# A two-pass cross-attention layer in float32: last denominators on VectorE, low-rank products in row groups, a key fold in the head

## The chip, the core and the metric

The kernel runs on one core of a Trainium2 chip. The core has five engines with queues of their own: TensorE (PE) multiplies matrices, VectorE (DVE) and ScalarE (ACT) work element by element and read TensorE's results from PSUM (8 banks of 128 x 512 float32), GpSimd (POOL) does small element work, and SyncE (SP) issues most of the DMA. They wait for each other through semaphores. The metric is the device time of one execution in microseconds.

## The reference

x is 128 latent rows of 256. The context has 12544 rows of 256. In float32:

```
x = x + cross_attention(layernorm(x), ctx)      # 16 heads of 64
    q = LN(lat) Wq;  k, v = LN(ctx) Wkv
    p = softmax(clip(q k^T / 8, -11, 11));  out = (p v) Wo + bo
x = x + self_attention(layernorm(x))            # 16 heads of 16
    Q, K, V and the output: y W^T + b + 2 (y A^T) B^T, A and B of rank 8
x = x + ffn(layernorm(x))                       # row-scaled fp8 values times fp8 weights
```

Nearly all the work is the cross-attention of the 128 latent rows with 12544 context rows.

## The kernel before

**Cross-attention.** The context is cut into 98 key tiles of 128 rows, 49 pairs. The 16 heads are done in two passes of 8 (`PASSES`), each over all pairs (`passes`, L266). Pair 0 and pairs 41 to 48 are written out, pairs 1 to 40 are a loop. Weights are folded once with the layer norm: for keys, Wk is folded (`key_fold`, L520) and multiplied with q to `qk_hi` and `qk_lo`; for values `value_fold`. Every float32 operand is split in a high and a low part, so a product is three matmuls (`mm3`, L456). A step is one key tile: on TensorE `values`, two times `scores`, and `weighted_sum` of the tile before (L488); ScalarE takes the exponentials (`exps`), VectorE clips them (`clip`), ScalarE and VectorE make their high and low parts (`p_high`, `p_low`), and VectorE adds them to `den` (`add_den`, L1021).

**Side work.** Steps of pairs 41 to 48 carry one extra piece each, numbered by `step_of` (L278). In pass 0 these make the second half's weights: key folds (`KEY_STEPS`), products with q (`QK_STEPS`), value folds (`VALUE_STEPS`). In pass 1 they project pass 0's heads, and one (`LORA_STEP`) scales the low-rank A. Before the passes stands the head: loads, layer norm of x, the first half's folds, the first tile.

**The end.** Behind the last tile, `denominators` (L506) turns `den` and the last tile's `ex` into one column per head: matmuls with a 128 x 128 stationary operand and a single moving column. `save` adds the high and low sums on VectorE (L1159), `inverse` takes the reciprocals (L1163), `project` multiplies each head with Wo (L516), and `add_head` adds the scaled result to x1 on VectorE (L1170), each addition waiting for the one before. Self-attention then needs the weights W + 2 B A: an identity matmul `weights_plain` (L662) puts W in PSUM and `weights_lora` (L668) adds the low-rank product; ScalarE copies the result (`effective_weights`, L911). Then: normalised rows (`hn`, L969), their transposes (L696), q and k (`projected`, L680), scores (L715, four row groups), exponentials (L920, L924), transposes (`transposed_probs`, L726), v projection (L734), products with v (L744), output projection (L757), and the fp8 layer. VectorE decodes the fp8 weights in between (`fp8_weights`).

The order on every engine is the order in which the code is written; no scheduler changes it.

Of the kernel before, what the change touches and what calls it, by code (L numbers as in the profile page):

```python
# [23 lines left out]
def perceiver_layer(  # L24
# [30 lines left out]
    with ExitStack() as stack:  # L55
# [13 lines left out]
        WO_BANK = (bank[4], bank[5], v_bank, side_bank)  # L69
# [67 lines left out]
        aa_all = sb("aa_all", [R, 4 * D])  # L137
        aa = [aa_all[:, n * D:(n + 1) * D] for n in range(4)]
        abT = [sb(f"abT{n}", [R, D]) for n in "qkvo"]
# [120 lines left out]
        AW_BANK = (3, 0, 3, 2)  # L260
# [22 lines left out]
        KEY_STEPS, QK_STEPS, VALUE_STEPS = range(0, 2), range(2, 6), range(6, 8)  # L283
        DEN_STEP, WO_STEPS, LORA_STEP = 0, range(1, 1 + HP), 1 + HP
# [21 lines left out]
        def _(sp):  # L306
# [39 lines left out]
            for n, (w, a, b_) in enumerate(((aWq, aAq, aBq), (aWk, aAk, aBk), (aWv, aAv, aBv), (aWo, aAo, aBo))):  # L346
                late_loads += [(aw[n][:, :, :], rows(w)), (aa[n], a), (abT[n][:, :], b_)]
# [107 lines left out]
        def _(pe):  # L455
# [50 lines left out]
            def denominators(dst, by_head, start, stop):  # L506

                for h in range(HP):
                    ins = pe.matmul(dst[:, h:h + 1], by_head[:, h, :], ones_sq[:, 0:1], start=start and h == 0,  # L509
                                    stop=stop and h == HP - 1)  # L510
                if stop:
                    ins.then_inc(s_denp, 1)

# [81 lines left out]
            pe.wait_ge(s_qT, CH + 1)  # L595

            def pair(p, i, phase):
                gp = p * PAIRS + i
                static = isinstance(i, int)
                for b in range(2):  # L600
# [19 lines left out]
                    if p == 0 and extra in KEY_STEPS:  # L620
                        if extra == 0:
                            pe.wait_ge(s_wk[1], 16)
# [680 lines left out]
```

## Time and profile before

| | |
|---|---|
| median of 3 runs | 1081.56 us (1081.37 to 1081.64) |
| profiled execution | 1076.75 us, its span 1075.0 us |
| busy in the span | TensorE 99%, VectorE 86%, ScalarE 61%, GpSimd 16% |
| mean granted clock of TensorE | 0.995 of 2.4 GHz |

How to read it: one execution was recorded. Times count from the start of the span. A timeline row gives start, length, engine, line, operation, output and inputs, and in brackets the idle time before it with what ended it. "x8" is eight instructions merged; a float32 matmul of the program is two instructions here, a transpose one. Matmuls overlap and their ends are modelled, so the pace of a run is read from starts, or from the chain of waits, which counts each stretch of time once.

### The profile page before, as it was taken

How to read it: one execution, taken by the hardware profiler on the slowest of the kernel's cores; microseconds unless marked ns; L12 is line 12 of the kernel's file. 1: busy time of each engine (PE TensorE's matmuls, PEld its weight loads, DVE VectorE, ACT ScalarE, POOL GpSimd, SP SyncE). 2: the span in 40 equal slices, each digit the busy share in tenths (PEclk: the TensorE clock that was granted, in tenths of full speed). 3: DMA queues.
4: the chain of work that ended last, by engine and by line, in shares of the span. 5: the costliest groups of instructions: out<-in, count | busy, mean ns of one | idle time of the engine just before them, and what ended most of it. 6: DMA issues, size and time to landing. Idle time of an engine off the chain costs nothing.

```text
span 1075.0 us, 18235 instructions
## 1 busy us (share of the span) xinstructions
PE 1065.5 (99%) x5510; PEld 906.0 (84%) x5510; DVE 926.8 (86%) x1321; ACT 660.8 (61%) x934; POOL 171.6 (16%) x213
## 2 busy tenths in 40 slices
PE   8999999999999999999999999999999999999998
PEld 6888888888888888888888888888888888888876
DVE  4999999999999999888888888888888888888864
ACT  4666666666666666565666666666666666666632
POOL 3233233233232232212000000000000000000000
PEclk9999999999999999999999999999999999999998
DMA  5321221221222212221151111111111111110000
GB/s 181 114 75 49 73 73 49 73 69 53 73 61 61 73 56 66 87 73 43 50 123 45 29 44 44 29 44 43 30 44 38 35 44 33 41 44 16 1 1 5
DMA packets 52509, 58.78 MB, mean 55 GB/s; under 512 B 31170, under 2 KB 32772, under 8 KB 52356
## 3 DMA queue, kind: packets, MB, share of 16 engines
q1 hardware_dynamic: 52052, 57.80, 18.5%
q10 hardware_dynamic: 432, 0.66, 0.2%
q8 instruction: 14, 0.23, 0.1%
q14 instruction: 11, 0.09, 0.0%
HBM read 58.20 MB, written 0.13 MB: 54 GB/s over the span
## 4 chain that ended last, share of the span: by engine, by line
PE 98%; DVE 1%; ACT 0%; issue 0%; POOL 0%; DVEq 0%; POOLq 0%
PE wide L458 25%; PE wide L459 25%; PE wide L460 25%; PE wide L499 17%; PE wide L516 1%; PE wide L523 1%; PE wide L530 1%; PE wide L509 0%; PE wide L545 0%; PE wide L551 0%; PE wide L538 0%; PE wide L744 0%; PE wide L680 0%; PE wide L668 0%; PE wide L726 0%; PE wide L662 0%
## 5 line engine op out<-in xcount | busy, mean ns | idle before, releaser
L816 ACT ACTIVATE ex<-wide,c_rstd 128x512 f32<-128x512 f32 x392 | 270.3, 690 | 201.3 <-PE wide L460 200.2
L458 PE MATMUL wide<-qk_hi,d_hi 128*128 128x512 f32 x784 | 305.2, 389 | 0.0
L460 PE MATMUL wide<-qk_hi,d_lo 128*128 128x512 f32 x784 | 305.0, 389 | 0.0
L459 PE MATMUL wide<-qk_lo,d_hi 128*128 128x512 f32 x784 | 305.0, 389 | 0.0
L1018 DVE TENSOR_TENSOR ph<-ex,ph 128x1024 fp32r<-128x1024 f32 x195 | 239.0, 1225 | 73.7 <-ACT ph L823 73.6
L823 ACT CAST ph<-ex 128x1024 fp32r<-128x1024 f32 x195 | 205.3, 1053 | 148.6 <-DVE ex L1000 148.6
L1027 DVE TENSOR_TENSOR den_all<-den_all,ex 128x1024 f32<-128x1024 f32 x193 | 234.6, 1215 | 0.0
L499 PEld LDWEIGHTS wide<-ph,vhl 128*128 128x128 f32 x1568 | 212.7, 190 | 16.6 <-DVE ph L1018 2.1
L499 PE MATMUL wide<-ph,vhl 128*128 128x256 f32 x1568 | 218.9, 282 | 0.0
L458 PEld LDWEIGHTS wide<-qk_hi,d_hi 128*128 128x128 f32 x784 | 147.1, 188 | 31.8 <-DVE qk_lo L1032 0.3
L459 PEld LDWEIGHTS wide<-qk_lo,d_hi 128*128 128x128 f32 x784 | 147.2, 188 | 30.8
L460 PEld LDWEIGHTS wide<-qk_hi,d_lo 128*128 128x128 f32 x784 | 147.1, 188 | 30.5
L1000 DVE TENSOR_SCALAR ex<-ex 128x1024 f32<-128x1024 f32 x195 | 135.1, 693 | 33.7 <-ACT ex L816 25.2
L458 PE MATMUL wide<-wv_hi,d_hi 128*128 128x512 f32 x392 | 158.3, 404 | 1.7 <-DVE vhl L989 1.7
L459 PE MATMUL wide<-wv_lo,d_hi 128*128 128x512 f32 x392 | 154.7, 395 | 0.0
L460 PE MATMUL wide<-wv_hi,d_lo 128*128 128x512 f32 x392 | 152.7, 390 | 0.0
L989 DVE SCALAR_TENSOR_TENSOR vhl<-wide,c_rstd,vhl 128x512 fp32r<-128x512 f32 x196 | 146.0, 745 | 3.1 <-ACT vhl L809 3.1
L809 ACT ACTIVATE vhl<-wide,c_rstd 128x512 fp32r<-128x512 f32 x196 | 133.6, 681 | 6.3 <-PE wide L460 6.0
L411 POOL TENSOR_TENSOR sig_all<-c_veps,half_pow 128x2 f32 (+1 forms) x49 | 46.0, 939 | 357.3 <-DVE c_veps L980 357.3
L417 POOL COPY c_rstd<-rstd_all 128x2 f32 (+1 forms) x49 | 26.7, 545 | 458.9 <-ACT ex L816 458.9
L460 PEld LDWEIGHTS wide<-wv_hi,d_lo 128*128 128x128 f32 x392 | 73.7, 188 | 17.0
L458 PEld LDWEIGHTS wide<-wv_hi,d_hi 128*128 128x128 f32 x392 | 74.3, 190 | 12.6 <-issue 2.6
(163 smaller groups left out, 636.0 us busy)
## 6 DMA issues: line engine op xcount, KB each, us to landing
t_all<-in_ctxT_dram SPq DMA_DIRECT2D x98, 384.0 KB, 3.1
x_pair<-in_ctx_dram SPq DMA_DIRECT2D x49, 256.0 KB, 2.7
diff<-sig_all SPq DMA_DIRECT2D x194, 0.5 KB, 1.9
wkv<-in_Wo_dram SPq DMA_DIRECT2D x2, 1024.0 KB, 10.1
wq<-in_Wq_dram SPq DMA_DIRECT2D x2, 512.0 KB, 7.7
wkv<-in_Wv_dram SPq DMA_DIRECT2D x2, 512.0 KB, 6.5
wkv<-in_Wk_dram ACTq DMA_DIRECT2D x1, 512.0 KB, 4.7
wkv<-in_Wk_dram SPq DMA_DIRECT2D x1, 512.0 KB, 3.6
```

What stands on the lines that cost most here:

```text
L411: pool.tensor_tensor(sig_all[:, pair_cols], c_veps[s][:, :], half_pow[:, :], ALU.pow).then_inc(s_sig, 1)
L458: pe.matmul(dst, hi, mhi, start=start, stop=False)
L459: pe.matmul(dst, hi, mlo, start=False, stop=False)
L460: return pe.matmul(dst, lo, mhi, start=False, stop=stop)
L499: ins = pe.matmul(acc[m][:, a, :, :], vhl[b][:, 2 * m + a, :, :].rearrange("p n d -> p (n d)"), ph[b][:, place(m, a), :, :], start=start a ...
L809: act.activation(vhl[b][:, :, 0, :], v_bank[:, :].rearrange("p (h d) -> p h d", h=HP), ACT.Identity, scale=c_rstd[s4][:, b:b + 1]).then_in ...
L816: act.activation(ex[b][:, c * HC:(c + 1) * HC, :], sc_bank[c][:, :].rearrange("p (h q) -> p h q", h=HC), ACT.Exp, scale=c_rstd[s4][:, b:b ...
L823: act.copy(ph[b][:, :, 0, :], ex[b][:, :, :]).then_inc(s_phi, 1)
L989: dve.scalar_tensor_tensor(vhl[b][:, :, 1, :], v_bank[:, :].rearrange("p (h d) -> p h d", h=HP), c_rstd[s4][:, b:b + 1], vhl[b][:, :, 0, : ...
L1000: dve.tensor_scalar(ex[b][:, :, :], ex[b][:, :, :], EXP_LO, EXP_HI, ALU.max, ALU.min).then_inc(s_clip, 1)
L1018: dve.tensor_tensor(ph[b][:, :, 1, :], ex[b][:, :, :], ph[b][:, :, 0, :].bitcast(F32), ALU.subtract)\
L1027: dve.tensor_tensor(den[p], den[p], ex[b][:, :, :], ALU.add).then_inc(s_den, 1)
```

## The change

- **Head.** `key_fold(1, CHUNK_M[0], side_bank)` and ScalarE's `key_weights` for it move from the first extra step of pass 0 to the end of the head; the load of Wk's second half moves in front of the sigma rows on SP. All later extra steps of pass 0 come one step earlier.
- **Denominators.** VectorE adds the last tile's `ex` to `den[1]` in two halves (`add_den_last`), and TensorE does 8 one-column matmuls, 4 ahead of and 4 behind the last weighted sum. The identity matmul for the q weights is issued ahead of them.
- **Low-rank products.** The A and B of q, k, v and o lie on partitions 0, 32, 64 and 96, and all eight matmuls are issued together behind the projections, for bank 7, 1, 2 and 3; the identity matmuls of k, v and o add to them later. A is scaled by four small operations in four steps.
- **Banks and order.** The last projections go to banks 4, 5, 6, 0 and 4 again (`WO_DST`); the v projection comes before the transposes of the probabilities; `save` comes before `inverse`; the fp8 decoding comes behind VectorE's copies of the transposes.

TensorE at the end of the program, before, from the last weighted sum but one (L499) over denominators (L509), projections (L516), identity matmuls (L662) and low-rank products (L668) to q and k (L680):

```order
L499 MATMUL wide<-ph,vhl 128x256 x8
L509 MATMUL wide<-ones_sq,den_all 128x1 x8
L509 MATMUL wide<-ones_sq,ex 128x1 x8
L499 MATMUL wide<-ph,vhl 128x256 x8
L516 MATMUL wide<-wkv,osum 128x256 x8
L662 MATMUL wide<-awq,ident 128x512
L668 MATMUL wide<-abTq,aa_all 128x256 x2
L662 MATMUL wide<-awk,ident 128x512
L696 MATMUL wide<-ident,ex 128x128 x2
L668 MATMUL wide<-abTk,aa_all 128x256 x2
L680 MATMUL wide<-latT,x_pair 128x128 x8
```

The same place after (weighted sums L498, denominators L508, projections L521, low-rank products L672, identity matmuls L514, q and k L685):

```order
L498 MATMUL wide<-ph,vhl 128x256 x8
L514 MATMUL wide<-awq,ident 128x512
L508 MATMUL wide<-ones_sq,den_all 128x1 x4
L498 MATMUL wide<-ph,vhl 128x256 x8
L508 MATMUL wide<-ones_sq,den_all 128x1 x4
L521 MATMUL wide<-wkv,osum 128x256 x8
L672 MATMUL wide<-abT_all,aa_all 128x256 x8
L514 MATMUL wide<-awk,ident 128x512
L703 MATMUL wide<-ident,ex 128x128 x2
L514 MATMUL wide<-awv,ident 128x512
L685 MATMUL wide<-latT,x_pair 128x128 x8
L514 MATMUL wide<-awo,ident 128x512
```

Half of the one-column matmuls are gone and the rest stand on both sides of the weighted sum; the low-rank products are one group of eight, and the first identity matmul stands ahead of the denominators.

VectorE at the same place, before: clips (L1006), low parts of the probabilities (L1013), inverse, saves, heads (L1170):

```order
L1027 TENSOR_TENSOR den_all<-den_all,ex 128x1024
L1006 TENSOR_SCALAR ex<-ex 128x512 x2
L1013 TENSOR_TENSOR ph<-ex,ph 128x4x128 x2
L1163 RECIPROCAL rden<-wide 128x8
L1159 TENSOR_TENSOR osum<-osum,wide 128x2x128 x4
L1170 SCALAR_TENSOR_TENSOR x<-wide,rden,x 128x256 x8
```

After: clips (L1009), denominator additions (L1024), low parts (L1016), saves, inverse, heads (L1183):

```order
L1037 TENSOR_TENSOR den_all<-den_all,ex 128x1024
L1009 TENSOR_SCALAR ex<-ex 128x512 x2
L1024 TENSOR_TENSOR den_all<-den_all,ex 128x512
L1016 TENSOR_TENSOR ph<-ex,ph 128x4x128 x2
L1024 TENSOR_TENSOR den_all<-den_all,ex 128x512
L1172 TENSOR_TENSOR osum<-osum,wide 128x2x128 x4
L1176 RECIPROCAL rden<-wide 128x8
L1183 SCALAR_TENSOR_TENSOR x<-wide,rden,x 128x256 x8
```

Two additions of half the heads are new, one ahead of the low parts and one behind; the inverse stands behind the saves.

TensorE in the head, before, at the end of the first tile's values:

```order
L458 MATMUL wide<-wv_hi,d_hi 128x512
L459 MATMUL wide<-wv_lo,d_hi 128x512
L460 MATMUL wide<-wv_hi,d_lo 128x512
L458 MATMUL wide<-wv_hi,d_hi 128x512
L459 MATMUL wide<-wv_lo,d_hi 128x512
L460 MATMUL wide<-wv_hi,d_lo 128x512
```

After, with a key fold (L528) there:

```order
L457 MATMUL wide<-wv_hi,d_hi 128x512
L458 MATMUL wide<-wv_lo,d_hi 128x512
L459 MATMUL wide<-wv_hi,d_lo 128x512
L528 MATMUL wide<-foldT,wkv 128x256 x4
L457 MATMUL wide<-wv_hi,d_hi 128x512
L458 MATMUL wide<-wv_lo,d_hi 128x512
L459 MATMUL wide<-wv_hi,d_lo 128x512
```

The fold's four matmuls stand between the first and the second tile's values. ScalarE at this place, before:

```order
L788 ACTIVATE qT<-wide 128x512
L809 ACTIVATE vhl<-wide,c_rstd 128x8x64
L803 CAST d_hi<-diff 128x512
L823 CAST ph<-ex 128x8x128
L809 ACTIVATE vhl<-wide,c_rstd 128x8x64
L816 ACTIVATE ex<-wide,c_rstd 128x512 x2
```

After:

```order
L791 ACTIVATE qT<-wide 128x512
L812 ACTIVATE vhl<-wide,c_rstd 128x8x64
L806 CAST d_hi<-diff 128x512
L787 COPY wkE<-wide 128x512
L826 CAST ph<-ex 128x8x128
L812 ACTIVATE vhl<-wide,c_rstd 128x8x64
L819 ACTIVATE ex<-wide,c_rstd 128x512 x2
```

The copy of the folded weights (L787) stands ahead of the cast of the first probabilities.

The diff, cut to its core:

```diff
-        WO_BANK = (bank[4], bank[5], v_bank, side_bank)
+        WO_DST = [bank[n][:, a * D:(a + 1) * D] for n, a in ((4, 0), (4, 1), (5, 0), (5, 1), (6, 0), (6, 1), (0, 0), (4, 0))]
+        aa_all, abT_all = (sb(n, [P, D]) for n in ("aa_all", "abT_all"))
+        aa, abT = ([t[32 * n:32 * n + R, :] for n in range(4)] for t in (aa_all, abT_all))
-        AW_BANK = (3, 0, 3, 2)
+        AW_BANK = (7, 1, 2, 3)
-        KEY_STEPS, QK_STEPS, VALUE_STEPS = range(0, 2), range(2, 6), range(6, 8)
-        DEN_STEP, WO_STEPS, LORA_STEP = 0, range(1, 1 + HP), 1 + HP
+        KEY_STEP, QK_STEPS, VALUE_STEPS = 0, range(1, 5), range(5, 7)
+        DEN_STEP, WO_STEPS, LORA_STEPS = 0, range(1, 1 + HP), range(1 + HP, 5 + HP)
...
+            sp.dma_start(wkv[:, 0, 1, :, :], Wk[:, 1, :, :]).then_inc(s_wk[1], 16)
             for n in range(1, 3):
                 sp.wait_ge(s_sig, n + 1)
                 sp.wait_ge(s_diff, n + 1)
                 sigma_row(n % 2, n)
-            sp.dma_start(wkv[:, 0, 1, :, :], Wk[:, 1, :, :]).then_inc(s_wk[1], 16)
...
             pe.wait_ge(s_qT, CH + 1)
+            pe.wait_ge(s_wk[1], 16)
+            key_fold(1, CHUNK_M[0], side_bank)
...
                     if ended:
+                        pe.wait_ge(s_late, LATE)
+                        weights_plain(0, True)
                         pe.wait_ge(s_vlo, ALL)
-                        pe.wait_ge(s_den, ALL - 1)
-                        denominators(v_bank, den[1], True, False)
-                        pe.wait_ge(s_clip, ALL + 1)
-                        denominators(v_bank, ex[b], False, True)
+                        pe.wait_ge(s_den, ALL)
+                        denominators(v_bank, den[1], 0)
                     weighted_sum(gp, b, first, last, saved=p * MH if first else 0, ended=ended)
+                    if ended:
+                        pe.wait_ge(s_den, ALL + 1)
+                        denominators(v_bank, den[1], 1)
...
+            def weights_lora():
                 for k in range(KD):
+                    for n in range(4):
+                        ins = pe.matmul(bank[AW_BANK[n]][:, k * D:(k + 1) * D], aa[n][:, k * P:(k + 1) * P], abT[n],
+                                        start=(k == 0 and n > 0), stop=(k == KD - 1 and n == 0))
...
                 for a in range(2):
-                    project(1, m, a, WO_BANK[m][:, a * D:(a + 1) * D])
+                    if (m, a) == (MH - 1, 1):
+                        pe.wait_ge(s_x1, 1 + HP + 2)
+                    project(1, m, a, WO_DST[2 * m + a])
...
+            def add_den_last(c):
+                heads = slice(c * HC, (c + 1) * HC)
+                dve.wait_ge(s_clip, ALL + c)
+                if c == 0:
+                    dve.wait_ge(s_den, ALL - 1)
+                dve.tensor_tensor(den[1][:, heads, :], den[1][:, heads, :], ex[1][:, heads, :], ALU.add).then_inc(s_den, 1)
...
+                        add_den_last(0)
                         p_low_last(g, b)
+                        add_den_last(1)
...
-            inverse(1, v_bank)
             save(PASSES - 1)
+            inverse(1, v_bank)
```

## Rows read from the trace of the kernel before

**Rows 1.** Table of stretches: us, busy and instructions by engine, clock, DMA share, GB/s.
```profile
100.00:1000.00 900.00, 900.00 (x4626) 768.30 (x4625) 796.56 (x1086) 572.79 (x798) 140.60 (x166) 1.00 0.19 53
1031.00:1036.00 5.00, 4.79 (x43) 4.59 (x41) 2.50 (x7) 2.10 (x6) 0.00 (x0) 1.00 0.01 3
1036.20:1039.50 3.30, 3.30 (x9) 2.55 (x9) 1.62 (x4) 0.04 (x1) 0.00 (x0) 0.50 0.00 0
1039.60:1046.30 6.70, 5.81 (x21) 3.37 (x21) 4.82 (x14) 0.59 (x1) 0.56 (x1) 1.00 0.00 1
1046.40:1049.70 3.30, 3.30 (x15) 2.92 (x14) 1.43 (x5) 1.21 (x3) 0.00 (x0) 0.50 0.00 0
1063.50:1066.80 3.30, 3.30 (x14) 2.94 (x13) 0.84 (x2) 0.00 (x0) 0.00 (x0) 0.50 0.00 0
```

**Rows 2.** Timeline, TensorE, 436 to 458: start, length, engine, line, operation.
```profile
440.95 1.12 PE L499 MATMUL wide<-ph,vhl 128*128 128x256 f32 x8
...
446.01 1.12 PE L499 MATMUL wide<-ph,vhl 128*128 128x256 f32 x8
...
452.82 1.11 PE L499 MATMUL wide<-ph,vhl 128*128 128x256 f32 x8
```

**Rows 3.** Timeline of the head, 24 to 29 us.
```profile
24.56 0.40 PE L460 MATMUL wide<-wv_hi,d_lo 128*128 128x512 f32 x1
...
26.09 1.05 ACT L823 CAST ph<-ex 128x1024 fp32r<-128x1024 f32 x1
...
26.69 0.47 PE L458 MATMUL wide<-wv_hi,d_hi 128*128 128x512 f32 x1 [1.73 <-DVE vhl L989]
...
28.60 1.21 DVE L1018 TENSOR_TENSOR ph<-ex,ph 128x1024 fp32r<-128x1024 f32 x1
```

**Rows 4.** SP's timeline, then the view of line 314, 0 to 30 us.
```profile
6.67 0.48 SPq L314 DMA_DIRECT2D t_all<-in_ctxT_dram  x1
...
DMA to landing us min/median/max: 7.6/9.1/10.0
```

**Rows 5.** Chain of waits from 1028 us: start, length, engine, tile, line.
```profile
1031.19 3.47 PE wide L509 x32
...
1035.92 5.42 PE wide L516 x16
...
1042.08 0.49 DVE x L1170
...
1042.69 0.50 DVE x L1170
...
1045.19 0.44 PE wide L696 x2
1045.62 1.23 PE wide L668 x4
1046.85 3.41 PE wide L680 x16
...
1051.12 1.08 PE wide L715 x16
...
1057.67 1.02 PE wide L726 x8
1058.69 3.48 PE wide L744 x32
```

**Rows 6.** Timeline at the last pair's end, VectorE and ScalarE.
```profile
1030.68 0.75 DVE L1006 TENSOR_SCALAR ex<-ex 128x512 f32<-128x512 f32 x2
...
1031.84 1.29 DVE L1013 TENSOR_TENSOR ph<-ex,ph 128x512 fp32r<-128x512 f32 x2 [0.41 <-ACT ph L830]
...
1035.04 1.20 ACT L838 COPY osum<-wide 128x256 f32<-128x256 f32 x4 [2.71 <-PE wide L499]
...
1035.44 1.41 DVE L1159 TENSOR_TENSOR osum<-osum,wide 128x256 f32<-128x256 f32 x4 [0.54 <-ACT osum L838]
```

**Rows 7.** Timeline of ScalarE, 1056.5 to 1058.6.
```profile
1056.74 0.67 ACT L924 ACTIVATE wq<-wq 128x512 f32<-128x512 f32 x1
```

More of the change, by code:

```diff
@@ L504, in weighted_sum, with denominators, weights_plain @@
                     ins.then_inc(s_pv, 1)
[L506 to L511, printed above, removed]
-                    ins.then_inc(s_denp, 1)
+            def denominators(dst, by_head, c):
+                for h in range(c * HC, (c + 1) * HC):
+                    ins = pe.matmul(dst[:, h:h + 1], by_head[:, h, :], ones_sq[:, 0:1], start=(h == 0), stop=(h == HP - 1))
+                if c == CH - 1:
+                    ins.then_inc(s_denp, 1)
+            def weights_plain(n, first):
+                ins = pe.matmul(bank[AW_BANK[n]][:, :], ident[:, :], aw[n][:, :, :].rearrange("p k d -> p (k d)"),
+                                start=first, stop=not first)
+                if not first:
+                    ins.then_inc(s_awp[n], 1)
             def project(p, m, a, dst):
@@ L644, in pair @@
                         pe.wait_ge(s_wvlo, KD * PASSES)
-                        denominators(side_bank, den[0], True, True)
+                        for c in range(CH):
+                            denominators(side_bank, den[0], c)
                     if p == 1 and extra in WO_STEPS:
@@ L718, in _ @@
                         ins.then_inc(s_ascore, 1)
-            weights_lora(2)
-            weights_plain(3)
-            weights_lora(3)
+            pe.wait_ge(s_awE[2], 1)
+            for k in range(KD):
+                pe.matmul(bank[1][:, 0:D], hT[:, k, :], awE[2][:, k, :], start=(k == 0), stop=False)
+            pe.matmul(bank[1][:, 0:D], ones_row[:, :], abv_row[:, :], start=False, stop=True).then_inc(s_avp, 1)
             def transposed_probs(n):
@@ L729, in _ @@
             transposed_probs(0)
+            pe.wait_ge(s_av, 1)
             transposed_probs(1)
-            pe.wait_ge(s_awE[2], 1)
-            pe.wait_ge(s_aexp, 1)
-            for k in range(KD):
-                pe.matmul(bank[4][:, 0:D], hT[:, k, :], awE[2][:, k, :], start=(k == 0), stop=False)
-            pe.matmul(bank[4][:, 0:D], ones_row[:, :], abv_row[:, :], start=False, stop=True).then_inc(s_avp, 1)
             pe.wait_ge(s_awE[3], 1)
@@ L928, in _ @@
             effective_weights(1)
+            effective_weights(2)
             act.wait_ge(s_aqp, 1)
             for m in range(KD):
-                ins = act.activation(aqT[:, m, :], bank[1][:, (2 + m) * P:(3 + m) * P], ACT.Identity,
+                ins = act.activation(aqT[:, m, :], bank[5][:, m * P:(m + 1) * P], ACT.Identity,
                                      bias=abq_col[:, m:m + 1], scale=1.0)
             ins.then_inc(s_aqT, 1)
+            effective_weights(3)
             self_exp(0)
-            effective_weights(2)
-            self_exp(1)
-            self_exp(2)
-            effective_weights(3)
-            self_exp(3)
             act.wait_ge(s_avp, 1)
             act.wait_ge(s_const, 6)
-            act.copy(av[:, :, 0:AD], bank[4][:, 0:D].rearrange("p (h d) -> p h d", h=AH)).then_inc(s_av, 1)
+            act.copy(av[:, :, 0:AD], bank[1][:, 0:D].rearrange("p (h d) -> p h d", h=AH)).then_inc(s_av, 1)
+            for n in range(1, 4):
+                self_exp(n)
             act.wait_ge(s_apTp, 3)
```

68 lines of the change are left out of this document (29 added, 39 removed).

## The prediction

> **What bounds the kernel now.** I read first the table of stretches. From 100 to 1000 us TensorE is busy for every microsecond at the full clock, so in the loops only work taken off TensorE counts [rows 1]. In the last 45 us the same view shows two other things: TensorE is not always busy, and its granted clock falls to 0.50 (1.2 instead of 2.4 GHz) in three stretches [rows 1]. Then the chain of waits of the tail, for what lies on the path there: the denominators (32 instructions, 3.47 us), the last projections (5.42), a chain of additions on VectorE, the wait for the normalised rows, the q and k projections (3.41), the scores, the transposes and the products with v (3.48) [rows 5]. Last the timeline, at the two places where instructions are moved: the head at 24 to 29 us [rows 3] and the end of the last pair of key tiles [rows 6].
>
> **The key fold in the head.** A step of the loop takes 446.01 - 440.95 = 5.06 us, and one that also carries a key fold 452.82 - 446.01 = 6.81 [rows 2]. So one fold costs 1.75 us, 0.219 for each of its 8 instructions, and with one step fewer in pass 0 this goes from a stretch that TensorE bounds. In the head the fold is put where TensorE stands still: the last values matmul starts at 24.56, so its successor could go at about 24.79, and the next one starts at 26.69, released by VectorE's `vhl` [rows 3]. That is 1.90 us for 1.75 us of work. ScalarE has one copy more there, about 0.6 us (half of the 1.20 us of four small copies is the nearest in size [rows 6]; bound 1.05, the large cast [rows 3]), in front of the cast of the first probabilities. The cast ran from 26.09 to 27.14; behind the fold's end (26.6) and the copy it runs from about 27.3 to 28.35, and VectorE asks for it only at 28.60 [rows 3]. So the head costs 0 (between -0.2, as a matmul that starts without a pause saves its ramp, and +0.2). The fold needs the second half of Wk in the head. Its load is put before the sigma rows in SP's queue, behind a load issued at 6.67; the slowest of the loads there took 10.0 us to land [rows 4]. Issued at 7.2 it lands by 17 to 18, against 24.8 when it is needed, and the sigma rows behind it have until 25.6. If that cover failed, TensorE and behind it ScalarE would wait. **Term 1: -1.75.**
>
> **The last denominators.** Now 32 instructions take 3.47 us, before the weighted sum can go [rows 5]. The change adds the last tile's exponentials on VectorE, so 16 stay, 1.74 us, in two halves around the weighted sum. Ahead of them goes an identity matmul (2 instructions, 0.86 us, as the chain has between q/k at 1050.26 and the scores at 1051.12 [rows 5]). VectorE: both clips end at 1031.43; an addition of half the heads is taken at 0.65, half of the 1.29 us of the two subtractions of the same size; it ends at 1032.08, the two subtractions at 1033.37, the second addition at 1034.02 [rows 6]. The subtraction thus comes 0.24 later than its 1031.84, which TensorE doesn't see. TensorE: identity matmul 1031.1 to 1032.0, first half of the denominators 1032.1 to 1032.97, weighted sum (8 instructions, 1.12 with the modelled end [rows 2], so 0.98) to 1033.95, second half 1034.07 to 1034.94. Before, the weighted sum started at 34.66. ScalarE's copies of the sums start 0.38 behind that start, now 1033.36; VectorE's four additions (1.41 [rows 6]) now wait for its second denominator addition, 1034.02 to 1035.43, ahead of TensorE all the same. Queued behind that addition on VectorE are the saves, the inverse and all heads, so it is what sets the pace if TensorE is quick.
>
> **The projections.** They took 5.42 us for 16 instructions, because 3.3 us of them ran at half clock [rows 1, 5]; at 0.219 they take 3.50. The first pair is then done at 1035.82, and VectorE's eight additions to x follow at one per 0.61 us (1042.08 to 1042.69 [rows 5]): 1035.95 + 7 x 0.61 + 0.50 = 1040.75. Before, the last one ended at 1042.69 + 0.50 = 1043.19. **Term 2: -2.4** at full clock; without the clock it is bounded by the order of the work alone, -1.0 (start of the projections 1035.92 to 1034.94). The wait of the last projection for bank 4 costs nothing: two additions are over long before.
>
> **The low-rank products.** Sixteen instructions on 8 rows go at once in four row groups. Alone, four in one group take 1.23 [rows 5]; sixteen with 32 rows in four groups take 1.08 in the scores [rows 5]. Taken: 1.1 for all, bound above by 16 x 0.27 = 4.3 if they don't overlap. TensorE is through with projections at 1038.4, with these at 1039.7 and with the next identity matmul at 1040.6, while the normalised rows come at 1045.19 - 2.4 = 1042.75. So they are hidden; at 4.3 the transposes would be 0.9 late. The late loads and the scaling of A are long done in either kernel, and the four small scalings lie in steps where VectorE has room.
>
> **From the rows to the scores.** Now from 1045.19 to 1051.12 + 1.08 = 1052.20, 7.0 us: the low-rank product 1.23 stands in it, and q and k take 3.41 at half clock [rows 1, 5]. After: transposes 0.44, identity matmul 0.86, q and k 16 x 0.108 = 1.73 (pace of 3.47/32), identity matmul 0.86, scores 1.08: 4.97. VectorE's k halves (0.9) fit beside the identity matmul. **Term 3: -2.0**; at half clock again only -0.3.
>
> **From the scores to the products with v.** Now 58.69 - 52.20 = 6.5, and the last exponential ends at 1057.41 [rows 7], 5.2 behind the scores. The v projection no longer stands before the last transposes (their eight take 1.02 [rows 5], four 0.5). So the products start 5.7 behind. **Term 4: -0.8.** The fp8 decoding moves behind VectorE's copies of the transposes, beside the products, for which VectorE only waits. Its five 512-wide operations take at most 0.65 each, as the subtractions [rows 6], 3.2 in all, and start about 0.6 behind the products' start: nothing, at most 0.3 late.
>
> **The clock takes a part back.** In before, the clock stood low behind the one-column denominators, behind the wait for the normalised rows with a low-rank product, and from 1063.4 on behind the 17-column products [rows 1, 5]. The first two causes get smaller. The third gets larger: the products now follow transposes of 0.5 us with gaps for the exponentials between them, where identity and low-rank products stood. I take the low clock to begin in the middle of the products: some 17 of 32 at 0.213 (3.41/16) instead of 0.109, +1.8, and +0.7 as the short chain behind them is low throughout. **Term 5: +2.5**, bounds 0 and +4.4 (all 32 low: 3.3, and 1.1 behind them).
>
> TensorE: Matmul & The Clock Gate in the Trainium skill (HAM oscillation) puts the fall of the clock down to TensorE standing idle between bursts. By that rule the idle here, which stays short, would leave the products at full clock, and the sum without term 5 would be -7.0. The trace does not agree: the clock was low from 1063.5 behind 3.48 us of products without a pause [rows 1, 5].
>
> **Sum:** -1.75 - 2.4 - 2.0 - 0.8 + 2.5 = -4.5 us. Against the profiled execution's 1076.75 (span 1075.0, 1.75 around it) this is 1072.3. The median of the runs, 1081.56, lies 4.8 above the profiled one; I take the difference as the same in both kernels: 1077.1.
>
> **Rivals.**
> - The clock holds. No low stretch before or in the products: -7.0, 1074.6. For it: half of the one-column work goes, and the denominators stand apart. Against: the products alone brought it down in before. 17%.
> - More low clock than I take: low from the last exponentials through the end of the chain (+4.4), and perhaps also at the projections (+1.4): gain 1.2 to 2.6, 1079.0 to 1080.4. For it: in the softmax TensorE does only four pieces of 0.5 us in 4 us, and once low, thin products don't raise the clock. 21%.
> - The row groups don't overlap: the transposes 0.9 late, 1078.0. Against: the scores' 1.08 for sixteen. 5%.
> - The change doesn't do what it says in the head: Wk lands late, or ScalarE's copy pushes the probabilities, and term 1 is gone: 1078.8. 6%.
> - Slower than before: the gap before the normalised rows grows from 0.9 to 2.1 us (1040.6 to 1042.75). If the clock falls there and, with thin work after it, does not rise before the end, everything TensorE does there runs at half pace: transposes to scores about 9.8 (+2.8 against before's 7.0), the products 6.8 (+3.3), the chain behind them +1.1, in all +7.2, against terms 1 and 2 and 0.3 left of term 4, -4.5: +2.7, 1084.3. It decides from where the low clock takes 4.5 us more than it does in before. Against: dense work raised the clock after each low stretch here. 3%.
> - The forecast, with the low stretch somewhere between q/k and the end of the products (a low stretch on q and k costs 1.7 and spares the products a part of theirs, which comes to nearly the same time): 48%, own range 1075.5 to 1078.5.
>
> **Numbers.** 1077.1. The range takes in most of the clock's cases, 1074.4 to 1080.1. 0.2%, about what a measurement of this kernel can tell from no change, is 2.2 us, so faster means under 1079.4: forecast 48, clock holds 17, row groups 5, head 5, and two thirds of the second rival 14, 89 in all; same 8; slower 3.
>
> **What would show it.** Steps of pass 0: one of 6.81 instead of two. Head: TensorE without the pause at 24.8 to 26.7, and no later start of the first weighted sum. Tail: sixteen one-column instructions in two groups of 0.9; the projections at 0.22 each and clock 1.00; the last addition to x 2.4 earlier relative to the last pair; all low-rank products in 1.1; q and k in 1.73; the products with v partly at 0.21 each. Wrong is the forecast if the clock is 0.50 in the projections, or if the products with v are wholly at one clock.

## The result, and the profile after

| | before | after |
|---|---|---|
| median of the runs in the first comparison (us) | 1081.46 (4 runs, 1080.22 to 1081.64) | 1074.30 (4 runs, 1071.72 to 1075.77) |
| ratio | | 0.9934 [0.9911, 0.9956] |
| median in a second comparison (us) | 1080.41 (21 runs, 1077.02 to 1081.79) | 1076.42 (5 runs, 1074.62 to 1077.57) |
| ratio | | 0.9956 [0.9942, 0.9969] |
| first profiled execution (us), its clock | 1076.75, 0.995 | 1071.72, 0.996 |
| second profiled execution (us), its clock | 1080.32, 0.991 | 1076.47, 0.991 |

The change makes the kernel faster by 7.2 us in the comparison that the forecast was made for, and by 4.0 in the second. The forecast, 1077.1, is 2.8 above the 1074.3 of the first, and the range's low end, 1074.4, is 0.1 above it. The 1076.42 of the second comparison lies inside the range.

Both kernels vary by more than that from one execution to the next. All 9 executions of after lie between 1071.72 and 1077.57, median 1075.77; all 57 of before between 1076.75 and 1081.84, median 1080.81. Over all of them the gain is 5.0. The time goes with the granted clock: of the 41 executions of before that stand beside the experiments below, those at 0.989 and 0.990 took 1081.3 to 1081.8, those at 0.991 1080.1 to 1081.0, those at 0.992 1079.0 to 1080.0, the one at 0.993 took 1078.70 and the one at 0.995 1077.02. At the same granted clock the two kernels can be compared without it: at 0.991 before took 1080.1 to 1081.0 and after 1076.4 to 1077.6, at 0.993 1078.7 (2 runs) and 1074.6 to 1075.8 (4 runs), at 0.995 1076.8 and 1077.0 against 1073.3. That is about 3.5 us for the work alone; what a median shows beyond it comes from which executions it was taken over.

First the steps of the prediction, in after's first profiled execution. Timeline of TensorE in the two kernels, before and then after: the first weighted sum of the program, and the first one of the last pair of tiles.

```profile
30.86 1.11 PE L499 MATMUL wide<-ph,vhl 128*128 128x256 f32 x8
...
1030.07 1.12 PE L499 MATMUL wide<-ph,vhl 128*128 128x256 f32 x8
```

```profile
30.98 1.12 PE L498 MATMUL wide<-ph,vhl 128*128 128x256 f32 x8
...
1028.55 1.12 PE L498 MATMUL wide<-ph,vhl 128*128 128x256 f32 x8
```

The loops are 1.64 us shorter, by the fold that is gone from them; the head is 0.12 longer. What hides the fold there, on all engines of after [rows 3]:

```profile
24.72 0.39 PE L459 MATMUL wide<-wv_hi,d_lo 128*128 128x512 f32 x1
...
24.95 1.89 PE L528 MATMUL wide<-foldT,wkv 128*128 128x256 f32 x8
...
26.75 0.50 PE L457 MATMUL wide<-wv_hi,d_hi 128*128 128x512 f32 x1
...
27.41 1.05 ACT L826 CAST ph<-ex 128x1024 fp32r<-128x1024 f32 x1
...
28.75 1.21 DVE L1028 TENSOR_TENSOR ph<-ex,ph 128x1024 fp32r<-128x1024 f32 x1
```

The values matmul behind the fold starts at 26.75 (26.69 before). ScalarE's cast starts 1.32 later than before and still ends at 28.46, before VectorE asks for it at 28.75. The fold costs the head nothing.

The chain of waits of after's tail [rows 5]:

```profile
1030.67 1.02 PE wide L508 x8
1031.69 1.06 PE wide L498 x8
1032.75 0.79 PE wide L508 x8
1033.54 5.26 PE wide L521 x16
...
1040.12 0.49 DVE x L1183
...
1042.61 0.44 PE wide L703 x2
1043.05 0.86 PE wide L514 x2
1043.91 1.78 PE wide L685 x16
1045.69 0.86 PE wide L514 x2
1046.56 1.11 PE wide L722 x16
...
1053.36 3.48 PE wide L747 x32
...
1059.79 1.53 PE wide L760 x4
...
1067.35 0.48 DVE lat L1263
```

Half the one-column matmuls are gone, 1.02 and 0.79 us stand on both sides of the weighted sum, and q and k (L685) take 1.78 instead of 3.41. But the projections (L521) still take 5.26, as before's 5.42: they are at half clock again. The products with v (L747) are at full clock. The table of stretches of after says the same (us, busy and instructions of TensorE, its weight loads, VectorE, ScalarE and GpSimd, clock, DMA share, GB/s) [rows 1]:

```profile
100.00:1000.00 900.00, 900.00 (x4625) 768.26 (x4624) 798.40 (x1089) 573.46 (x799) 142.16 (x166) 1.00 0.19 53
1033.80:1037.00 3.20, 3.20 (x9) 2.57 (x8) 1.18 (x4) 0.00 (x0) 0.00 (x0) 0.50 0.00 0
1037.20:1057.40 20.20, 17.04 (x121) 11.99 (x119) 13.56 (x33) 7.28 (x18) 0.55 (x1) 1.00 0.00 1
1057.60:1060.90 3.30, 3.30 (x14) 3.03 (x14) 0.42 (x1) 0.00 (x0) 0.00 (x0) 0.50 0.00 0
```

Two low stretches are left before the final chain where before had three: the one on the low-rank product and q/k is gone. The timeline of VectorE in after [rows 6]:

```profile
1029.84 0.68 DVE L1024 TENSOR_TENSOR den_all<-den_all,ex 128x512 f32<-128x512 f32 x1
1030.44 1.29 DVE L1016 TENSOR_TENSOR ph<-ex,ph 128x512 fp32r<-128x512 f32 x2
1031.64 0.68 DVE L1024 TENSOR_TENSOR den_all<-den_all,ex 128x512 f32<-128x512 f32 x1
1032.48 1.41 DVE L1172 TENSOR_TENSOR osum<-osum,wide 128x256 f32<-128x256 f32 x4 [0.15 <-ACT osum L841]
```

The added operations take 0.68 each (0.65 was taken) and the saves run beside TensorE. The sixteen low-rank products, in TensorE's timeline of after, the line that answers to the 1.23 us for four [rows 5]:

```profile
1038.72 1.15 PE L672 MATMUL wide<-abT_all,aa_all 8*128 8x256 f32 x16
```

They do overlap: 1.15 for all sixteen.

Now the same kernel, executed again. Its stretches:

```profile
1042.30:1045.60 3.30, 3.30 (x16) 3.22 (x16) 0.00 (x0) 1.21 (x3) 0.00 (x0) 0.50 0.00 0
1045.70:1052.30 6.60, 5.22 (x36) 2.90 (x34) 5.11 (x11) 3.67 (x11) 0.00 (x0) 1.00 0.00 1
1052.50:1066.10 13.60, 13.60 (x58) 12.37 (x57) 4.32 (x11) 1.03 (x2) 0.00 (x0) 0.50 0.00 1
```

and of its chain of waits the first ten projections (all sixteen took 3.70 in the timeline), q and k, and the products:

```profile
1033.40 2.28 PE wide L521 x10
...
1042.80 3.19 PE wide L685 x16
...
1054.11 6.64 PE wide L747 x32
```

The code is the same, and the time is 1076.47 instead of 1071.72. Here the projections are at full clock, q and k and all the products at half. In before the low stretches began at the same three places in both profiles; in after no low stretch belongs to a fixed instruction. From start to start of the same steps, in the two pairs of profiled executions:

| us | first pair | second pair | forecast |
|---|---|---|---|
| up to the last pair's first weighted sum | -1.52 | -1.92 | -1.75 |
| from there to the end of the additions to x | -1.05 | -2.15 | -2.4 |
| to the end of the scores | -1.96 | -1.93 | -2.0 |
| to the start of the products with v | -0.80 | -0.37 | -0.8 |
| from there to the end | +0.31 | +2.54 | +2.5 |
| sum | -5.02 | -3.83 | -4.45 |

The second pair is close to the forecast line by line, but in part by luck: the forecast was worked out from before's first execution, and before's second one has longer low stretches. Against the first one the second execution of after has -0.32 in the third row and +4.3 in the fifth, which are the prediction's values for q and k at half clock (-0.3) and for low clock from the products to the end of their chain (+4.4). In the first pair the low clock lay in the projections, so the second row is 1.35 short of the forecast, and not in the products, so the last row costs 2.2 less. The two misses cancel in part.

### The profile page after: what moved, and what is told of

Its sections match the earlier page's. It is cut to its first block, busy times and chain, and to the rows that moved or that the text cites. A ratio compares the mean times of both kernels' runs of the same rounds, so it can differ in the third digit from the quotient of the medians.

```text
span 1070.0 us, 18208 instructions
## 1 busy us (share of the span) xinstructions
PE 1059.8 (99%) x5494; PEld 901.2 (84%) x5494; DVE 928.6 (87%) x1326; ACT 660.9 (62%) x934; POOL 173.0 (16%) x213
## 4 chain that ended last, share of the span: by engine, by line
PE 97%; DVE 2%; ACT 0%; issue 0%; POOL 0%; DVEq 0%; POOLq 0%
PE wide L457 25%; PE wide L458 25%; PE wide L459 25%; PE wide L498 17%; PE wide L521 1%; PE wide L528 1%; PE wide L535 1%; PE wide L550 0%; PE wide L556 0%; PE wide L543 0%; PE wide L508 0%; PE wide L747 0%; DVE a_max L1222 0%; PE wide L680 0%; PE wide L685 0%
## 5 line engine op out<-in xcount | busy, mean ns | idle before, releaser
L498 PEld LDWEIGHTS wide<-ph,vhl 128*128 128x128 f32 x1568 | 212.6, 190 | 16.7 <-DVE ph L1028 2.1
L498 PE MATMUL wide<-ph,vhl 128*128 128x256 f32 x1568 | 219.0, 282 | 0.0
```

The costliest lines, as they stand in the source:

```text
L498: ins = pe.matmul(acc[m][:, a, :, :], vhl[b][:, 2 * m + a, :, :].rearrange("p n d -> p (n d)"), ph[b][:, place(m, a), :, :], start=start a ...
```

## Experiments: two executions of each kernel, and the two halves of the change

Before, unchanged.

> The kernel before, unchanged, to see its executions with their clocks. The profiled executions of the two kernels differ by 5.0 us, the medians by 7.2, so 2.1 us lie between executions. Clock theory: executions of one kernel differ by how many low-clock stretches fall on TensorE's work; each lowers the mean granted clock by about 0.0016 and costs up to 1.7 us, so a time of 1081.5 goes with a clock near 0.992 and one of 1077 with 0.995, and its trace shows low stretches that the first profiled execution did not have. Rival (a fixed cost outside TensorE's clock, in loads or in the head): times spread by the same amount with the clock the same.

Measured: 1080.43 (11 runs, 1078.35 to 1081.76) beside 1080.41, ratio 0.9996 [0.9987, 1.0005]. The profiled execution took 1080.32, 3.57 more than the first. Its low stretches:

```profile
1036.00:1039.20 3.20, 3.02 (x7) 2.48 (x8) 1.83 (x6) 0.50 (x2) 0.00 (x0) 0.50 0.00 0
1046.20:1052.80 6.60, 6.60 (x21) 4.36 (x20) 2.62 (x9) 1.21 (x3) 0.00 (x0) 0.50 0.00 0
1063.30:1069.90 6.60, 6.60 (x23) 5.55 (x24) 1.11 (x3) 0.00 (x0) 0.00 (x0) 0.50 0.00 0
```

They begin where the first profile's did [rows 1], but the second and the third last twice as long. So the clock theory's account of the spread held, with 0.990 instead of 0.992 for the executions at 1081.5. The first profiled execution of before was the fastest of all 57; 44 of the 57 are above 1080. The forecast rests on it.

After, unchanged.

> The changed kernel, unchanged. Clock theory: executions from 1071.5 to 1076, each on one line of time against mean clock (0.996 to 0.993, about 1.1 us for 0.001), and a trace with another number of low stretches than the first, or with them at other places; median 1074.3, 7.2 below before. Rival (the gain is all work taken off the path, 7 us, and the first pair of profiles was a poor pair): the trace shows the parts of work adding up to 7 without regard to the clock.

Measured: 1076.42 (5 runs), ratio 0.9956 [0.9942, 0.9969]; its rows are above. The expected median of 1074.3 was missed by 2.1, and one execution, 1077.57, lies above the expected span. The profiled execution stood 2.6 below its own median in the first comparison and at its median in the second.

Only the head's edit, with the load of Wk's second half, in before.

```diff
+            key_fold(1, CHUNK_M[0], side_bank)      # TensorE, end of the head
+            key_weights(CH, CHUNK_M[0], side_bank)  # ScalarE, end of the head
-        KEY_STEPS = range(0, 2)
+        KEY_STEP = 0
```

> The kernel before with only the key fold moved into the head. By steps of the loop -1.75, by the first pair of profiles -1.5: 1.5 to 1.8 us faster than before at the same clock. Rival (the fold is not hidden in the head): 0 faster. If it moves by more than 2, the moved phase of the tail against the clock's stretches has a share.

Measured: 1078.88 (11 runs, 1078.38 to 1079.67), ratio 0.9986 [0.9977, 0.9995]: -1.5, close to the 1.75 of term 1. From the first weighted sum to the last pair's it takes 997.59 us, as after (997.57 and 997.56), against 999.21 and 999.34 in before.

Only the tail's edits: after with the fold and the load of Wk's half back in their old places.

```diff
-            key_fold(1, CHUNK_M[0], side_bank)
-        KEY_STEP, QK_STEPS, VALUE_STEPS = 0, range(1, 5), range(5, 7)
+        KEY_STEPS, QK_STEPS, VALUE_STEPS = range(0, 2), range(2, 6), range(6, 8)
```

> The changed kernel with the key fold put back into the loop, so only the tail is changed. The work theory gives the rest of the gain: 7.2 - 1.6 = 5.6 below before in the median, 3.5 below at equal low stretches. If tail and head don't add up to the whole (within 0.7 us), the clock's phase decides the rest.

Measured: 1076.97 (5 runs, 1076.17 to 1078.89), ratio 0.9964 [0.9951, 0.9978]: -3.4. The expected 5.6, which came from the first comparison's 7.2, was missed; the 3.5 expected at equal low stretches fits. The halves add up to -5.0 where the whole gives -4.0 in the same comparison. The missing 1.0 is less than the 3.0 between the executions of after there, so it says nothing of the two edits getting in each other's way.

## Experiments: can the low clock be taken away?

If the clock makes the difference between executions, a kernel in which it stays high must be faster and vary less, with the same work on the path. Four kernels, all made from after.

Denominators 64 columns wide instead of 1.

```diff
-                    ins = pe.matmul(dst[:, h:h + 1], by_head[:, h, :], ones_sq[:, 0:1], ...)
+                    ins = pe.matmul(dst[:, h * DH:(h + 1) * DH], by_head[:, h, :], ones_sq[:, 0:DH], ...)
```

> The changed kernel; the denominator matmuls move 64 columns of ones instead of one (64 equal results a head, one is read). The pace of such a float32 instruction is 0.109 us with 1 or with 128 columns, so no work is added to the path. Clock theory (thin matmuls bring the clock down): the low stretch that the first profiled execution of the changed kernel had in the projections (1033.6 to 1037.0) does not occur in any execution; in the executions where it did not fall there anyway nothing changes. Median 0 to 1 us below the changed kernel (1075.8 over nine executions), fastest not changed. Rival (only idle time brings it down): no difference.

Measured: 1075.82 (6 runs, 1071.90 to 1077.47), ratio 0.9945 [0.9929, 0.9961]. The eight instructions take about as long as with one column (1.08 and 1.02). The profiled execution (1076.55) has no low stretch in the projections, but one from 1042.5 and then this one:

```profile
1052.80:1066.40 13.60, 13.60 (x57) 12.27 (x56) 4.31 (x12) 0.82 (x2) 0.00 (x0) 0.50 0.01 1
```

These are the places of after's second execution, which has one-column denominators. The medians of that one, 1076.42, and of this kernel differ by less than either spreads: alone this edit brings nothing that shows. Whether the low stretch in the projections is gone from every execution, as the clock theory has it, one profile can't tell.

The products with v also wider, 32 columns a head instead of 17 (the rest are ones, not read).

```diff
-                ins = pe.matmul(bank[5][:, h * (AD + 1):(h + 1) * (AD + 1)], a_pT[:, at, :], av[:, h, :], ...)
+                ins = pe.matmul(bank[5][:, h * 2 * AD:(h + 1) * 2 * AD], a_pT[:, at, :], av[:, h, :], ...)
```

> As den_wide, and the products with v move 32 columns instead of 17 (the rest are ones; not read). Clock theory: the products hold the clock a little better, 0 to 2 us on the median, since in the second profiled execution of the changed kernel the low clock lay over all of them (1052.5 to 1066.3). Rival: as den_wide.

Measured: 1073.04, but from 1070.12 to 1077.49 in 5 runs, ratio 0.9922 [0.9909, 0.9935]. The profiled execution is the slowest of the five, and its clock fell twice: from 1040.1 to 1047.0, beginning while TensorE waited for the normalised rows and lying on q and k (3.41 us), and from 1053.8 to 1067.5, so from the end of the softmax, in which TensorE also waits, and ahead of the wide products. Of its chain:

```profile
1055.12 6.67 PE wide L747 x32
```

The median is 2.8 below that of the kernel with wide denominators alone, but the intervals of the two ratios overlap.

Fillers: after's shapes, with products of the identity with itself that nobody reads where TensorE waits ahead of the products with v, written to a bank that is free there: 5 (10 instructions) ahead of the normalised rows, and 1 or 2 between the transposes of the probabilities. The helper `busy` for them is in both kernels already, with 2, 2 and 16 of them behind the products with v. The identity matmul for the k weights is also held back here until the sixth addition to x.

```diff
+            pe.wait_ge(s_x1, 1 + HP + 6)
             weights_plain(1, False)
+            busy(bank[6], 5)
             pe.wait_ge(s_hn, 1)
...
+            busy(bank[2], 2)
             transposed_probs(0)
+            busy(bank[2], 1)
             transposed_probs(1)
+            busy(bank[3], 2)
             transposed_probs(2)
+            busy(bank[3], 1)
             transposed_probs(3)
```

> The changed kernel with 128-column matmuls of the identity into free banks where TensorE only waits: five while it waits for the normalised rows, and 2, 1, 2 and 1 ahead of the four groups of transposes. They cost at most some 0.2 us each where they overrun a wait. Clock theory: the low stretches on q and k and at the start of the products go, the spread of executions (1071.7 to 1077.6) shrinks and the median falls by 2 to 4 us, to 1072 to 1074. Rival (the gain of the change is work alone, and the clock's state is outside the kernel's hands): +0 to +1 us, same spread.

Measured: 1071.78 (5 runs, 1070.21 to 1072.45), ratio 0.9911 [0.9898, 0.9924]. In the profiled execution the clock is high up to 1055.4, in the last third of the products, and low first there:

```profile
1052.71 4.04 PE wide L753 x32
```

The kernel is 4 us faster than the median of after's nine executions, and as much faster than the kernel with wide denominators alone (1075.82), which was timed in the same comparison. It does all of after's work and more, so the rival, that only work counts, is out. The fillers and the identity matmul that was held back were not tried apart.

All three together.

> fillers and den_av_wide together. Clock theory: 1071 to 1073.5 and a spread under 3 us, faster than the changed kernel by 2 to 5; trace with low stretches only at the products' end or behind. Rival: as the changed kernel, 1075.8.

Measured: 1070.14 (4 runs, 1069.17 to 1070.39), ratio 0.9902 [0.9888, 0.9917]: 10.7 us less than before, and the fastest kernel here. Its profiled execution, 1069.17, has no low stretch at all. The three others took 1070.1 to 1070.4 at a mean clock of 0.997 and 0.998, so the clock fell in them too; where isn't recorded. Its stretches, and of its chain the products and a later group, which is L760 in after:

```profile
1029.30:1058.50 29.20, 27.84 (x193) 21.83 (x193) 19.83 (x47) 9.69 (x25) 0.55 (x1) 1.00 0.01 1
1058.60:1067.40 8.80, 4.39 (x37) 3.75 (x35) 5.14 (x17) 0.37 (x1) 0.59 (x1) 1.00 0.04 15
```

```profile
1052.12 3.49 PE wide L753 x32
...
1057.62 1.15 PE wide L766 x4
```

TensorE is busy for 27.84 of 29.20 us. Products of 32 columns take 3.49, those of 17 took 3.48; L766 takes 1.15 where L760 took 1.53 and 1.75 in after. The spread between executions is 1.2 us (4 runs) instead of 5.9 (9 runs). This shows that most of the spread of after, and 4 to 6 us of its time, are the clock's. Most of that came with the fillers: the two wide shapes add 1.6 by the medians, and the intervals of the two ratios overlap, so that they help at all is not shown here.

## Experiments: the edits, undone in the kernel with all three means

The same means in before: wide denominators, wide products and three fillers ahead of the normalised rows.

> The kernel before with the means that held the clock in all_warm, as far as it has places for them: denominators with 64 columns, products with v with 32, three 128-column identity matmuls in the wait for the normalised rows. Clock theory: most of all_warm's 10.7 us is the clock, so this kernel gains 4 to 7 us over before without any of the change's edits: 1074 to 1077. Rival (the change's order is what keeps the clock up): 0 to 2 us faster. What is left to all_warm's 1070.1 is the change's work: fold 1.5 to 1.75, denominators and projections about 1, low-rank product between hn and q/k 0.4, v projection 0.8, in all 3.7 to 4.0, so 1074 if the clock holds wholly.

Measured: 1074.32 (5 runs, 1073.73 to 1075.95) beside 1081.52, ratio 0.9938 [0.9924, 0.9951]: -7.2 without any edit of the change, a little more than the 4 to 7 expected. Which of the three means did it in this kernel was not tried. The profiled execution is its slowest, 1075.95 at a clock of 0.997; three of the others were at 1.000. Its stretches and its denominators (32 instructions of 64 columns, in the timeline):

```profile
1030.00:1047.60 17.60, 16.72 (x99) 13.45 (x98) 12.60 (x31) 4.89 (x10) 0.55 (x1) 1.00 0.01 1
1047.80:1051.00 3.20, 3.20 (x12) 2.06 (x10) 1.16 (x3) 0.62 (x2) 0.00 (x0) 0.50 0.00 0
```

```profile
1032.40 1.90 PE L509 MATMUL wide<-ones_sq,den_all 128*128 128x64 f32 x16
1034.13 1.95 PE L509 MATMUL wide<-ones_sq,ex 128*128 128x64 f32 x16
```

The projections are at full clock in this kernel too, and from the last pair's first weighted sum to the end of the additions to x it takes 11.88 us, against 10.85 in the kernel with all three means. That is 1.03 for the order of the work alone, where the prediction gave -1.0. Between the two kernels lie 4.2 us by their medians (3.9 by their ratios), but not at the same clock: most executions of this kernel were at 1.000 and most of the other's below. At 1.000 it took 1073.73 to 1074.32 (3 runs) and the other 1069.17 (1 run), so 4.6 to 5.2 apart. The prediction's terms without the clock are 1.75, 1.0, 0.3 and 0.8, together 3.85, near the 3.5 between before and after at equal clock and below this.

Then each edit undone in the kernel with all three means (1070.14 in 4 runs). That kernel was timed in the comparison before this one, on another chip, and in the kernels below the clock fell behind the products in the profiled execution, where in its own it did not. So the differences of the medians hold some clock too; the profiles and the executions at equal clock say more.

The fold back in the loop:

> all_warm with the key fold back in the loop. With the clock held the price of the fold stands alone: +1.5 to +1.75 against all_warm's 1070.1. Rival (the fold's gain in the first pairs was partly the clock's phase): +1.0 or less.

Measured: 1072.84 (5 runs, 1070.81 to 1073.29), ratio 0.9923 [0.9907, 0.9938]: +2.7, above the expected 1.5 to 1.75, though the intervals of the two ratios overlap. The profiled execution is 3.7 slower than the other kernel's: the additions to x end 2.3 later, of which 0.4 was lost in the head already, and the clock is low from 1058.5, behind the products, which makes the other 1.3 at the end. The one execution at 1.000 took 1070.81, 1.64 more than the other kernel's 1069.17 at that clock: the price of the fold as expected.

All 32 denominators on TensorE, ahead of the weighted sum, and no additions on VectorE:

```diff
-                        denominators(v_bank, den[1], 0)
+                        denominators(v_bank, den[1], True, False)
+                        pe.wait_ge(s_clip, ALL + 1)
+                        denominators(v_bank, ex[b], False, True)
...
-                        add_den_last(0)
                         p_low_last(g, b)
-                        add_den_last(1)
```

> all_warm with the last tile's denominators by TensorE again (32 instructions ahead of the weighted sum, 64 columns each). At full clock the first pair of projections ends 1.6 us later than in all_warm (start 35.2 instead of 33.6), and VectorE's eight additions follow at the same pace: +1.4 to +1.7. Rival (VectorE's two extra additions cost what they save): +0.5 or less.

Measured: 1073.34 (5 runs, 1070.86 to 1073.94), ratio 0.9922 [0.9905, 0.9938]: +3.2, above the expected 1.4 to 1.7, with overlapping intervals again. The last addition ends 2.0 later in the profiled execution. That is 1.03 as found above, and 0.86 for the identity matmul, which now stands in front of the 3.52 us of denominators instead of where TensorE would wait: a reading, no run has the one without the other. The rest of the 4.2 between the profiles is a low stretch from 1057.6 behind the products. Its two executions at 0.999 took 1070.86 and 1071.52, 1.7 and 2.4 above 1069.17.

The low-rank products in one row group, and no filler ahead of the normalised rows:

```diff
-        aa_all, abT_all = (sb(n, [P, D]) for n in ("aa_all", "abT_all"))
-        aa, abT = ([t[32 * n:32 * n + R, :] for n in range(4)] for t in (aa_all, abT_all))
+        aa_all, abT_all = (sb(n, [P, 4 * D]) for n in ("aa_all", "abT_all"))
+        aa, abT = ([t[0:R, n * D:(n + 1) * D] for n in range(4)] for t in (aa_all, abT_all))
-            busy(bank[6], 5)
```

> all_warm with all A and B on partitions 0 to 7, so in one row group, and without the five fillers in the wait for the normalised rows, whose time these products take. In the trace 16 x 0.23 = 3.7 us for the products instead of 1.1, transposes 0.2 to 0.5 us late: +0.2 to +0.7 if the clock holds. If 8-row matmuls don't hold the clock, a low stretch on q and k, +1.7 and more. Rival (row groups bring nothing, the products overlap or not by another rule): 1.1 us in the trace again.

Measured: 1073.63 (5 runs, 1072.79 to 1074.17), ratio 0.9933 [0.9919, 0.9947]: +3.5, here with intervals that don't overlap, and the case expected for a clock that doesn't hold (+1.7 and more). The sixteen in the chain of waits, and the stretches at and behind them:

```profile
1037.80 3.65 PE wide L672 x16
```

```profile
1037.80:1041.40 3.60, 3.60 (x17) 2.84 (x17) 2.66 (x7) 0.59 (x1) 0.35 (x1) 1.00 0.00 0
1041.80:1045.10 3.30, 3.30 (x7) 1.34 (x6) 0.88 (x4) 0.59 (x1) 0.00 (x0) 0.50 0.00 0
```

In one row group they take 3.65, so the four groups save 2.5 us of TensorE's time there. The first row of the table of stretches is the more telling one: TensorE was busy for all of the 3.6 us before the clock fell. It fell behind instructions that use 8 of 128 rows, without a pause. That these eight-row instructions are the cause is not shown: the five fillers were taken out too, this is one execution, and in after, with four groups, the clock behind them stayed high in one profile and fell at 1042.2 in the other, 0.9 us behind a wait of 2.18 us. The low stretch lay on two identity matmuls (1.65 and 1.71 us instead of 0.86), not on q and k (1.82). Of the 3.9 us between the profiles 0.7 was lost before the last pair of tiles, 1.9 came from there to the products and 1.3 behind them, where the clock was low again from 1058.8.

TensorE: Matmul & The Clock Gate in the Trainium skill (Measured speedup vs the span model) gives 3.07 times for four row groups of 32 rows and 512 columns; here it is 3.65 / 1.15 = 3.2 times with 8 rows and 256 columns, so the runs come close to it.

## Why the prediction was wrong

Its terms for the work were nearly right; the step that turned them into a time was not.

- **Term 1, -1.75: right.** The loops gave 1.64 and 1.78 in the two pairs of profiles, the fold alone 1.5 in the medians and 1.6 between two executions at clock 1.000, and the head hid it as worked out, cast and load included.
- **Term 2, -2.4 at full clock, -1.0 by the order alone: right as two cases, and I took the wrong one for the first pair.** It was -1.05 there, as the projections ran at half clock again, and -2.15 in the second pair. That fewer one-column matmuls would keep the clock up is not shown either way: the same program had both. The sign named in the prediction for a failed forecast, a clock of 0.50 in the projections, did appear.
- **Term 3, -2.0: right**, -1.96 and -1.93. The row groups overlap (1.15; 1.1 was taken). In the first pair q and k went from 3.41 to 1.78, as forecast. In the second they still took 3.19, and the row came out alike because before's own execution was low for longer there.
- **Term 4, -0.8: right** in the first pair. In the second it was -0.37, since the low clock began during the last transposes.
- **Term 5, +2.5: mis-sized for the first pair, right for the second.** The low clock was to begin in the middle of the products. In the first profiled execution it began 0.7 us behind their end (+0.3), in the second it lay on all of them (6.64 us, +2.5 for this row, as the low stretch of before's second execution was longer too; +4.3 against the execution that the term was worked out from, near its upper bound of 4.4).
- **The failed step: "The median of the runs, 1081.56, lies 4.8 above the profiled one; I take the difference as the same in both kernels."** The sum gave 1072.3 for after's profiled execution, and that took 1071.72: right to 0.6, with luck, as term 2 was 1.35 too large and term 5 2.2 too large, with opposite signs. The 4.8 was then added. For before it was the distance between an execution with few low stretches, the fastest of 57, and its usual ones. It says nothing of a property that after must share: in after the four runs of the comparison lay 2.6 above its profile. Of the 2.8 us of error, 0.6 is the sum's and 2.2 this step's. Over all executions the two distances turned out equal after all, 1080.81 - 1076.75 and 1075.77 - 1071.72, 4.06 and 4.05; with nine executions of after instead of four the forecast would have been 1.3 too high and inside its range. So what failed is that single executions were taken as if they were numbers of the kernel; and that the median fell 0.1 below the range instead of inside it is the draw of four executions.
- **The range** was built from rivals on where the clock falls in one execution, and took the result as one number for each. A median of four executions of a kernel that varies by 5.9 us was not in it. The low end, 1074.6 for "the clock holds", stood for one that never came: with clocks of 0.991 to 0.996 the nine executions of after lie from 1071.72 to 1077.57, on both sides of it.
- **Rivals.** That the clock holds did not happen: the faster of the two profiles has two low stretches up to the end of the products' chain, and the other a longer one. That more of it is low happened in single executions (1077.57) and not in the median. The row groups and the head held. Slower than before was far off.

What stays open: what decides in which of the places the clock falls in one execution. The same program had its low stretch in the projections once and on q/k and the products another time, though its projections started at 1033.54 and 1033.40 and its first weighted sum was equal to 0.12 us. So neither the order nor the place of the work alone decides it, and what does was not tried.

## What to carry to other kernels

Read the granted clock of the profiled execution beside that of the timed runs before taking it as the base of a sum, and where they differ look for the low stretches; one profile of a kernel whose clock falls is one draw. Where TensorE waits in a chain of small matmuls, fill the waits with work that nobody reads: here that was worth 4 us, and together with wider matmuls 5.6 in after and 7.2 in before, as much as the whole change. Wider matmuls cost next to nothing here, but alone their gain didn't show. Spread small-row products over row groups. Judge edits of such a tail by executions at the same granted clock, where their own work shows without it; a kernel that mostly holds the clock gives more of them.

## What the runs showed of the hardware

- The same program differs by 4.8 us between two executions on the granted clock of its last 45 us alone, 1071.72 at 0.996 and 1076.47 at 0.991.
- The clock fell behind TensorE work without a pause: at 1063.4 in before, behind 3.48 us of 17-column products and 1.2 us of small matmuls, and at 1041.7 in one execution behind 3.65 us of products with 8 rows in one row group. It fell in or shortly behind a wait too: at 1040.1 with wide products, at 1042.2 in after's second execution.
- Instructions of 128 rows took nearly the same time whatever their columns, 1 or 64 (1.02 and 1.08 for eight; 3.47 and 3.52 for thirty-two), or 17 or 32 (3.48 and 3.49 for thirty-two). So wider ones cost at most 0.06 us a group here.
- The head varies too: the first weighted sum started between 30.84 and 32.17 in the profiled executions of all these kernels. In the two that were 1.2 and 1.3 later than before's, the first fold had waited 0.64 and 0.91 us for Wk to land.
- Work that nobody reads made the kernel faster: after's 1075.77 (median of nine) became 1071.78 with 11 small matmuls (22 instructions) in waits.
